# Sixteen-head attentions: values as stationary blocks of 32 columns, a turned result, and denominators summed by halvings on GpSimd

## The reference

```python
def xattn(q, k, v):                        # q: layernorm(x), k = v = context, 77 tokens
    qh, kh, vh = split(q @ Wq.T + bq), split(k @ Wk.T + bk), split(v @ Wv.T + bv)
    attn = jnp.einsum('bhqc,bhkc->bhqk', qh, kh) * 16 ** -0.5
    attn = jnp.where(mask == 0, -jnp.inf, attn)          # layer 0 alone
    attn = softmax(attn, axis=-1)
    out = jnp.einsum('bhqk,bhkc->bhqc', attn, vh)
    return merge(out) @ Wo.T + bo
x = x + tanh(g_xattn[0]) * xattn(layernorm(x), ctx, ctx)
```

## Time and profile before

| | |
|---|---|
| three runs | 1043.39, 1044.92, 1045.66 us; median 1044.92 |
| profiled execution, span | 1043.2 us |
| TensorE busy | 964.7 us (92%) |
| VectorE busy | 603.3 us (58%) |
| ScalarE busy | 489.0 us (47%) |
| GpSimd busy | 287.8 us (28%) |
| chain that ended last | TensorE 20% of the span, the last feed-forward block |

### The profile page before, as it was taken

How to read it: one execution, slowest core, us unless ns; L and a number is a source line. 1 busy time by engine, 2 the same in 40 slices (tenths; PEclk the granted TensorE clock), 3 DMA queues, 4 the chain that set the end, 5 groups by cost and what they waited for, 6 DMA issues and landing times. The chain is left out here.

```text
span 1043.2 us, 18151 instructions
## 1 busy us (share of the span) xinstructions
PE 964.7 (92%) x6476; PEld 835.3 (80%) x6477; DVE 603.3 (58%) x1253; ACT 489.0 (47%) x744; POOL 287.8 (28%) x271
## 2 busy tenths in 40 slices
PE   6999999989999999877988889999998999999997
PEld 5778878878888888565777778887885799999996
DVE  5858769951223222689898999666776522222221
ACT  3654422111111111688785878255552556656561
POOL 2000000033444442280006112600000344444442
PEclk9999999999999999998999999999999999999999
DMA  9200040025667664011000010260115223322332
GB/s 295 69 1 22 21 143 21 21 77 166 181 181 210 182 168 91 15 41 41 1 1 2 1 41 2 99 231 21 41 42 171 83 45 50 48 45 48 51 45 31
DMA packets 62500, 79.38 MB, mean 76 GB/s; under 512 B 7340, under 2 KB 46855, under 8 KB 62439
## 3 DMA queue, kind: packets, MB, share of 16 engines
q1 hardware_dynamic: 48807, 59.95, 17.0%
q0 software_dynamic: 13632, 18.62, 10.2%
HBM read 60.73 MB, written 17.83 MB: 75 GB/s over the span
## 5 line engine op out<-in xcount | busy, mean ns | idle before, releaser
L3165 PEld LDWEIGHTS ps<-room,xn_sb 128*128 128x128 f32 x1248 | 145.6, 192 | 2.7 <-issue 0.8
L3165 PE MATMUL ps<-room,xn_sb 128*128 128x128 f32 x1248 | 146.3, 275 | 0.6 <-issue 0.6
L288 POOL TENSOR_TENSOR norm_vec<-norm_vec,powers 128x4 f32<-128x4 f32 (+2 forms) x27 | 28.9, 1071 | 360.7 <-DVE norm_vec L282 360.7
L3118 POOL DMA_INDIRECT out_x<-f_yo,f_give x39 | 62.0, 1589 | 110.5 <-DVE f_yo L3363 97.5
L3234 ACT ACTIVATE xn_sb<-w_L_ffn_w 128x1024 f32 x78 | 82.1, 1057 | 20.8 <-DVE f_te L3331 10.8
L3357 DVE TENSOR_TENSOR room<-room,ps 128x512 f32<-128x512 f32 x39 | 26.8, 687 | 109.5 <-PE ps L3165 109.5
L2857 DVE TENSOR_TENSOR room<-room,ps 128x1024 f32<-128x1024 f32 x24 | 29.3, 1219 | 104.0 <-issue 89.5
L2461 PE MATMUL ps<-b_room,room 128*128 128x256 f32 x384 | 85.6, 380 | 3.7 <-DVE room L2857 1.6
L2461 PEld LDWEIGHTS ps<-b_room,room 128*128 128x128 f32 x384 | 72.6, 190 | 14.1 <-issue 1.8
L2673 ACT ACTIVATE room<-ps 128x1024 f32<-128x1024 f32 x24 | 24.6, 1023 | 115.2 <-PE ps L2441 115.2
L2418 POOL DMA_INDIRECT acc_rows<-f_eo,f_idx x32 | 52.4, 1637 | 94.7 <-DVE f_eo L2883 50.9
(11 more groups left out here) (404 smaller groups left out, 2059.4 us busy)
## 6 DMA issues: line engine op xcount, KB each, us to landing
w_L_ffn_w<-in_L_ffn_w SPq DMA_DIRECT2D x24, 512.0 KB, 9.8
b_room<-in_L_ffn_Wg SPq DMA_DIRECT2D x16, 512.0 KB
b_room<-in_L_ffn_Wu SPq DMA_DIRECT2D x16, 512.0 KB
b_room<-in_L_ffn_Wd SPq DMA_DIRECT2D x16, 512.0 KB, 6.3
xn_rows<-xn_sb SPq DMA_DIRECT2D x8, 512.0 KB, 2.9
x_sb<-in_x SPq DMA_DIRECT2D x4, 512.0 KB, 6.4
xn_sb<-in_L_ffn_w SPq DMA_DIRECT2D x2, 1024.0 KB, 7.6
x_sb<-acc_rows SPq DMA_DIRECT2D x4, 512.0 KB, 5.9
```

The source lines that it names most:

```text
L3118: pool.indirect_dma_start(out_rows[:, :], bass.IndirectOffsetOnAxis(ap=give[:, j:j + 1], axis=0), yo[j % 2][:, :], None, compute_op=ALU.ad ...
L3165: m = pe.matmul(ps[:, banks[p], f * P:(f + 1) * P], wb[p][:, n, i, f * P:(f + 1) * P], xsT[p][:, i * P:(i + 1) * P], start=(i == 0), stop= ...
```

## The change

- A head's weights are padded from 77 to 80 (`LP`), so that the 16 heads make 1280 columns, ten pieces of 128; the padding of `pr` is set to zero once.
- `values(n)` takes a block of `vblk` of 128 x 32 (two heads) as stationary and 128 columns of `pT` as moving side, and writes partitions 32i to 32i + 31 of the result. Sixteen matmuls in two phases; the late phase waits for the third eviction. The result comes out turned (features on partitions), so `turn_heads` and the copy to `oT` go away.
- The denominators no longer come from the ones. GpSimd adds the halves of `pr` per head, 80 to 40 to 20 to 10 (`denominators`, three additions over 640, 320 and 160 elements, into `sm`); VectorE sums the ten and takes the reciprocal (`inverse(n)`, first in its iteration n, ahead of `front(n+2)`); ScalarE copies the 16 reciprocals to 256 columns (`widen(n)`, behind the exponentials of n+1, ahead of the evictions of n); TensorE transposes these two blocks behind the last two of the weights, and one 128 x 512 eviction takes all four.
- `normalise(n)` is one multiplication of the result in PSUM by the turned reciprocals, straight into `oT`, which has two buffers.
- `project(n-1)` stands behind `turn(n, (0, 1))` instead of at the end of the iteration.
- Waits: the exponentials also wait for the first addition of two tiles before; the third eviction waits for the multiplication of the tile before, as `values(n)` does; `normalise(n)` waits for the projection of the tile before; `project(n)` for the residual of the tile before.
- `place_values` has 5 matmuls (128 or 256 columns) and 5 VectorE operations; `own` is masked by 2 operations of GpSimd instead of 20. The roots go between the denominators; the table `lanes` of layer 3 is filled at the end of GpSimd's program of the attention.

```diff
@@ tensor: turn, values @@
                         if r == 2:
                             pe.wait_ge(pt_sb, 3 * n + 1)
-                        elif n:
-                            pe.wait_ge(pt_sb, 3 * n)
...
+                            for half in range(2):
+                                lo = half * HALF + 4 * P
+                                pe.transpose(ps[:, 4, half * P:(half + 1) * P], pr[:, n % 2, lo:lo + P], K.ident[:, :])
+                            pe.wait_ge(r_wide, n + 1)
+                            for k in range(KT):
+                                m = pe.transpose(ps[:, 4, (2 + k) * P:(3 + k) * P], wide[:, k * P:(k + 1) * P], K.ident[:, :])
...
                 def values(n):
...
-                        pe.wait_ge(on_ready, n)
-                    for r, (lo, hi) in enumerate(rounds):
-                        pe.wait_ge(pt_sb, 3 * n + r + 1)
-                        for part in range(lo, hi):
-                            w, h = rows[part], head0[part]
-                            m = pe.matmul(ps[:, 6, h * HV:(h + 3) * HV], pT[0:w, n % 2, part, :],
-                                          vblk[0:w, n // TB, part, :, :].rearrange("p j c -> p (j c)"),
-                                          start=(part == 0), stop=(part == NC - 1), skip_group_check=True)
+                        pe.wait_ge(oT_sb, n)
+                    for late in range(2):
+                        for half in range(2):
+                            pe.wait_ge(pt_sb, 3 * n + (3 if late else half + 1))
+                            for i in range(4):
+                                q = i + late
+                                m = pe.matmul(ps[i * RG:(i + 1) * RG, 6, half * P:(half + 1) * P],
+                                              vblk[:, q, 2 * b + half, 0 if late or i == 0 else 1, :], pT[:, n % 2, half if q < 4 else 2, q if q < 4 else half, :],
+                                              start=(half == 0 and not late), stop=bool(late), skip_group_check=True)
                     m.then_inc(o_ready, 1)
...
                     turn(n, (0, 1))
                     if n:
-                        turn_heads(n - 1)
+                        project(n - 1)
...
-                    if n:
-                        project(n - 1)
@@ scalar @@
+                        act.wait_ge(s_den, 3 * (n - 2) + 1)
...
+                def widen(n):
+
+                    act.wait_ge(r_den, n + 1)
+                    if n:
+                        act.wait_ge(pt_ps, 3 * n)
+                    act.activation(wide[:, :].rearrange("p (h d) -> p h d", h=H),
+                                   rden[:, n % 2, :].unsqueeze(2).broadcast_to([P, H, HD]), ACT.Copy).then_inc(r_wide, 1)
...
+                    widen(n)
+                    for r in range(3):
                         act.wait_ge(pt_ps, 3 * n + r + 1)
                         if n >= 2 and r == 0:
                             act.wait_ge(o_ready, n - 1)
+                        if n >= 2 and r == 2:
+                            act.wait_ge(oT_sb, n - 1)
+                        act.activation(pT[:, n % 2, r, :, :].rearrange("p a b -> p (a b)"),
+                                       ps[:, 4 + r % 2, :], ACT.Copy).then_inc(pt_sb, 1)
@@ gpsimd @@
+                def denominators(n):
+
+                    def add(src, w):
+                        lo = H * (LP - 2 * w)
+                        to = sm[:, n % 2, lo:lo + H * w].rearrange("p (h k) -> p h k", h=H)
+                        pool.tensor_tensor(to, src[:, :, 0:w], src[:, :, w:2 * w], ALU.add).then_inc(s_den, 1)
+                        return to
+
+                    pool.wait_ge(p_ready, n + 1)
+                    forty = add(pr[:, n % 2, :].rearrange("p (h k) -> p h k", h=H), LP // 2)
+                    pool.wait_ge(s_den, 3 * n + 1)
+                    twenty = add(forty, LP // 4)
+                    pool.wait_ge(s_den, 3 * n + 2)
+                    add(twenty, LP // 8)
@@ vector @@
+                def inverse(n):
+
+                    lo = H * (LP - LP // 4)
+                    dve.wait_ge(s_den, 3 * n + 3)
+                    dve.tensor_reduce(den[:, n % 2, :], sm[:, n % 2, lo:lo + H * LP // 8].rearrange("p (h k) -> p h k", h=H), AX.X,
+                                      ALU.add).then_inc(s_sum, 1)
+                    dve.wait_ge(s_sum, n + 1)
+                    if n >= 2:
+                        dve.wait_ge(r_wide, n - 1)
+                    dve.reciprocal(rden[:, n % 2, :], den[:, n % 2, :]).then_inc(r_den, 1)
+
                 def normalise(n):
...
                     dve.wait_ge(o_ready, n + 1)
-                    dve.reciprocal(rden[:, n % 2, :], o[:, :, HD]).then_inc(n_step, 1)
...
+                        dve.wait_ge(y_ready, n - 1)
+                    dve.tensor_tensor(oT[:, n % 2, :], ps[:, 6, 0:D],
+                                      pT[:, n % 2, 2, 2:4, :].rearrange("p a b -> p (a b)"), ALU.mult).then_inc(oT_sb, 1)
...
                 for n in range(NT):
+                    inverse(n)
                     if n + 2 < NT:
                         front(n + 2)
```

More of the change, by code:

```diff
@@ L31 @@
 H, HD = 16, 16
-CHUNKS = -(-H * L // P)
+LP = 80
+PARTS = 5
+HALF = H * LP // 2
 LN_EPS = 1e-5
@@ L348, in multihead @@
     G2 = 2 * L
-    rounds = [(0, 4), (4, 8), (8, NC)]
+    PLACE = ((0, 6, 0), (1, 6, 128), (4, 6, 384), (2, 7, 0), (3, 7, 256))
     ps = K.ps
@@ L425, in place_values @@
                     again = K.again[:, :, :].rearrange("l h k -> l (h k)")
-                    for part in range(NC):
-                        w, h = rows[part], head0[part]
-                        m = pe.matmul(ps[0:w, 6 + part // HALF, part % HALF * 96:(part % HALF + 1) * 96].rearrange("p (b c) -> p b c", b=B),
-                                      again[:, part * P % L:part * P % L + w], vnat[:, :, h * HD:(h + 3) * HD], start=True, stop=True)
-                        if part % HALF == HALF - 1:
+                    for q, bank, at in PLACE:
+                        lo, hi = max(q - 1, 0), min(q + 1, 4)
+                        w = 4 * (hi - lo) * RG
+                        m = pe.matmul(ps[:, bank, at:at + w].rearrange("p (g c) -> p g c", g=2 * B),
+                                      again[:, q * P % LP:q * P % LP + P],
+                                      vnat[:, :, :].rearrange("l b (h c) -> l (b h) c", h=2)[:, :, lo * RG:hi * RG],
+                                      start=True, stop=True)
+                        if q >= 3:
                             m.then_inc(s_vp, 1)
@@ L489, in turn @@
                         m.then_inc(pt_ps, 1)
                 def values(n):
+                    b = n // TB
                     if n:
[L493 to L500 removed]
@@ L551, in _ @@
                 if first:
-                    pe.wait_ge(opening.again, 1)
+                    pe.wait_ge(opening.again, 2)
                 place_values()
@@ L719, in _ @@
                     opening.gpsimd(pool)
-                for b in range(B):
-                    m = pool.tensor_copy(vblk[:, b, :, :, HD].rearrange("p c j -> p (c j)"), K.own[:, :])
-                m.then_inc(s_vblk, 1)
-                for g in range(len(norm.groups)):
-                    if first or g:
-                        norm.root(pool, g)
-                if ahead is not None:
-                    ahead.gpsimd(pool)
+                pool.memset(pr[:, :, :].rearrange("p n (h k) -> p (n h) k", h=H)[:, :, L:LP], 0.0).then_inc(s_vblk, 1)
+                def denominators(n):
[10 more added lines that the diff above has]
+                    add(twenty, LP // 8)
+                if first:
+                    norm.root(pool, 0)
+                norm.root(pool, 1)
+                if ahead is not None:
+                    ahead.gpsimd_start(pool)
+                for n in range(NT):
+                    denominators(n)
+                    if first and n in (0, 2):
+                        norm.root(pool, 2 + n // 2)
+                    if ahead is not None:
+                        ahead.gpsimd(pool, n)
+                if ahead is not None:
+                    ahead.gpsimd_end(pool)
             @block.vector
@@ L1685, in rows_of_x, with gpsimd_start, gpsimd, gpsimd_end @@
         pass
-    def gpsimd(self, pool):
-        for g in range(len(self.GROUPS)):
-            self.norm.root(pool, g)
+    def gpsimd_start(self, pool):
+        pass
+    def gpsimd(self, pool, n):
+        for g, (_, hi) in enumerate(self.GROUPS[:4]):
+            if n == hi + 1:
+                self.norm.root(pool, g)
+    def gpsimd_end(self, pool):
+        self.norm.root(pool, 4)
     def vector(self, dve, n):
```

124 lines of the change are left out of this document (47 added, 77 removed).

## The result

The changed kernel takes 1054.25 us in the median of five runs (1051.89 to 1058.81) against 1045.1 for the kernel before; the ratio is 1.0089, with a 95% interval of 1.0071 to 1.0108. It is slower by some 9 us. The prediction of 1046.2 was wrong, and its range ended at 1054.0, just under the median. The profiled execution spans 1051.2 us, 8.0 more than before.

The account below looks back on a forecast made before the run. VectorE was taken to bind layer 0, with TensorE holding it up in layer 3. Terms -0.6 + 0.9 + 0.6 - 0.6 + 1.0 = +1.3; 1043.2 + 1.3 + 1.7 = 1046.2 us, range 1039 to 1054.

Parts of the forecast that it names:

- the one on GpSimd: GpSimd's halving adds beside VectorE: hidden themselves, slowing VectorE's small operations, mainly bias and moments, by +1.0 us in all.
- rival B: Layer 0's bias on VectorE waits for GpSimd's adds, up to 1.59 us each, 6 us in all: 1051; chance 0.12.
- rival C: Values on TensorE: four blocks don't all run together, late phase over 0.75, loop 0.25 longer: 1052; chance 0.21.
- Four tiles: Two plain tiles and two with extra transposes: 24.92 us for 25.12 in layer 0, 23.86 for 23.58 in layer 3.
- The loop: Per-tile cycle from inverse through ScalarE, TensorE and normalise back to the next inverse: 5.88 us, binding layer 3.
- the hops: Loop steps from inverse through widen, evictions, transposes and hand-overs to the late values phase: 3.69 us.
- VectorE's room: Layer 0 tiles: VectorE nearly always busy, so taking work off TensorE alone buys at most 0.2 us per tile.
- The tails: Each attention's last two tiles, without front: loop stays 5.88, once with moments taken at 0.9 more; +0.7 and +1.6.
- rival A: Both attentions: shorter hand-overs make the loop 5.6 us, no contention, -5.0 us in all: 1040 us; chance 0.25.
- From the last multiplication to the last residual: End of each attention: new chain 1.74 us instead of 3.71, -2.0.

Follow-up runs that it names:

- no_adds: Changed kernel without GpSimd's three halving additions per tile (one element written instead, VectorE sums ones; denominators left out): 1044.6 us, 0.9991 of the kernel before.
- rows_moved: Changed kernel with moments and normalised rows moved behind the next iteration's maximum and subtraction, roots one tile later: 1040.78 us, 0.9962 of the kernel before.
- bias_first: Changed kernel with moments and rows moved behind the next iteration's bias, and layer 3's table cast ahead of GpSimd's loop: 1035.72 us, 0.9912 of before.
- rows_two_inputs: Changed kernel with the normalised rows computed by an operation with two tensor inputs instead of one with two scalars: 1059.11 us, 1.0133 of before.

## Why the prediction was wrong, point by point

**The step that failed** is the one on GpSimd, "I take +1.0 us in all". It rests on "Only the bias (16 operations) and the moments have two operands in SBUF", and the rows were left out of the list because they have one tensor input and two columns of scalars. They stand in VectorE's order right behind the residual, where the exponentials have just ended and the additions begin; they are what the additions hit. The term measured 9.7 us (the changed kernel less `no_adds`, medians) instead of 1.0. Of the 15 us by which rows grew, 11.3 reached the end, by the residuals of both attentions.

The prediction had the mechanism as rival B, at 0.12, and gave it a price near the true one (6 us against 9.7), but tied it to the bias. The nearness is luck, as the price was worked out from 16 biases that weren't held. The bias collides just as hard when it is put there (1.77 us in `rows_moved`); it decided at another operation. The view that would have told was at hand: list VectorE's operations in the order of their start behind the end of the exponentials, for a tile with rows, and ask of each whether it could meet the addition, instead of going by operands.

The Trainium skill, "SBUF — State Buffer", section "Who interferes with whom", names the operation: beside those with two SBUF inputs it lists copies, casts and `tensor_scalar` as able to take the port pair that VectorE and GpSimd share, with whoever comes first keeping it for the whole instruction. The trace agrees (a row ends 0.15 us behind the addition's end; the row that came 0.27 ahead of one was not held). The prediction quoted half of that rule, and the half that it left out is the one that decided.

**What held.** Without the additions the forecast is 1046.2 - 1.0 = 1045.2; `no_adds` measured 1044.6. That the sum came out is in part luck, as two errors cancel in it: up to the thirteenth residual `no_adds` is 2.3 us shorter than before in layer 0 and 1.6 in layer 3 (forecast: 0.6 shorter and 0.9 longer), and behind it 3.1 and 2.7 longer (forecast: 0.3 each).
- TensorE's blocks run side by side: the 32 records of values take 1.40 us (1.3 forecast), four blocks of 32 columns at once, and the late phase 0.64 (0.65), so rival C's condition isn't met. These are the rows of after, of both phases and of the late one:

```profile
112.22 1.40 PE L503 MATMUL ps<-a_pT,a_vblk 128*32 128x128 f32 x32
...
112.98 0.64 PE L503 MATMUL ps<-a_pT,a_vblk 128*32 128x128 f32 x16
```

- The three additions take 1.55, 0.86 and 0.49, 2.9 us (2.8 forecast), and `inverse` never waits for them.
- `place_values` takes 1.91 us on TensorE (2.0).
- Four tiles in `no_adds`, from the sixth residual on: 24.71 us in layer 0 (24.92 forecast) and 23.29 in layer 3 (23.86).
- TensorE's busy share from 80 to 137 us was forecast at 85%; without the additions it is 47.29 of 57 us, 83%, and with them 79%.

**What was mis-sized.**
- The loop. The prediction read the 2.19 us from the multiplication to the next `front` off one tile and called it plain; that tile holds a pair of rows, 0.98 us. Without them it is 1.2, and with the 3.69 of the hops the loop is 4.89, which `bias_first` takes in its plain tiles. Its row of multiplication, residual, statistics and next inverse:

```profile
740.15 0.42 DVE L787 TENSOR_TENSOR a_oT<-ps,a_pT 128x256 f32<-128x256 f32 x1 [0.34 <-PE ps L503]
740.49 0.47 DVE L798 SCALAR_TENSOR_TENSOR x_sb<-ps,gates,x_sb 128x256 f32<-128x256 f32 x1
741.00 0.43 DVE L800 BATCH_NORM_STATS2 bn_st<-x_sb 128x6 f32<-128x256 f32 x1
741.34 0.30 DVE L775 TENSOR_REDUCE a_den<-a_sm 128x16 f32<-128x160 f32 x1
```

  The four-tile sums came out right, since in the changed order rows do stand in the loop.
- VectorE's room. "In layer 0 VectorE has no room" was read off the same tile. In a tile of the kernel before in which VectorE has neither rows nor moments, and TensorE has four extra transposes, VectorE idles 1.49 us from residual to residual (88.29 to 94.78), most of it at these two places:

```profile
89.67 1.44 DVE L744 TENSOR_REDUCE a_mx<-ps 128x16 f32<-128x1232 f32 x1 [0.43 <-PE ps L472]
...
94.78 0.48 DVE L770 SCALAR_TENSOR_TENSOR x_sb<-ps,gates,x_sb 128x256 f32<-128x256 f32 x1 [0.61 <-PE ps L516]
```

- The tails. The last two tiles were taken at 5.88 and 6.8. Without the additions they take 5.83 and 7.74 in layer 0 and 5.96 and 7.61 in layer 3: a pair of rows stands ahead of the last inverse, and not the moments alone. With the additions they take 7.62 and 7.20 in layer 0; there the first holds two held rows. With rows and moments moved (`bias_first`) they take 4.89 and 5.00. This error hid the gain: with the rows moved the change is worth 0.9%, which no case of the prediction held apart from rival A's 1040.
- From the last multiplication to the last residual: 143.09 - 140.97 = 2.12, forecast 1.74 (3.71 in the earlier trace rows); a pair of rows stands ahead of the last residual:

```profile
140.97 0.42 DVE L787 TENSOR_TENSOR a_oT<-ps,a_pT 128x256 f32<-128x256 f32 x1 [2.83 <-PE ps L503]
...
143.09 0.48 DVE L798 SCALAR_TENSOR_TENSOR x_sb<-ps,gates,x_sb 128x256 f32<-128x256 f32 x1
```

**What stays open.** The runs of `no_adds` lie in two groups, 1040.1 to 1040.6 and 1044.2 to 1047.4, and those of the changed kernel spread over 7 us. The half clock (next section) falls in other places from kernel to kernel, and its part in the 9 us wasn't measured by itself. A kernel without additions and with the rows moved wasn't run, so that the 8.9 us apart from the additions come from the last tiles is read off the two traces and not shown by an edit.

## What to carry to other kernels

Before work is given to an idle GpSimd, write down which VectorE operations start while it runs; those that read two tensors from SBUF may last until the GpSimd instruction ends, and so may a `tensor_scalar` or a copy with one. Move those operations to a stretch in which GpSimd rests, or put ones that aren't held into its additions, before judging the change: here the same work went from 0.9% slower to 0.9% faster by its order, about half of that because of the additions. And when a period is read off one tile, check that this tile has no work that others lack.

## What the runs showed of the hardware

- A VectorE operation of 0.41 to 0.48 us on SBUF that starts well within a GpSimd addition is not slowed in proportion: it lasts until the addition is over. With one tensor input and two scalars it ends 0.15 us behind the addition's end (a row of the changed kernel, 1.37 us), and so does a copy ahead of the loop (1.51 instead of 0.28); with two tensor inputs 0.28 behind (a row of `rows_two_inputs`, 1.51, and the bias in `rows_moved`, 1.77). A bias that starts in the last 0.11 us of an addition keeps its 0.43, and the GpSimd addition behind it takes 0.60 to 0.63 us instead of 0.49 (five times in the changed kernel).
- Not every operation on SBUF is held. The statistics of a residual, SBUF to SBUF, keep their 0.43 us inside the long addition (rows below, of after); in `bias_first` ten of the reductions of `inverse` and eleven of the reciprocals start inside an addition and keep 0.30 and 0.25.

```profile
66.45 1.54 POOL L725 TENSOR_TENSOR a_sm<-a_pr 128x640 f32<-128x640 f32 x1 [0.43 <-ACT a_pr L626]
...
66.56 0.43 DVE L800 BATCH_NORM_STATS2 bn_st<-x_sb 128x6 f32<-128x256 f32 x1
```

- A TensorE that waits can lose its clock. In layer 3 of the changed kernel TensorE sat idle for 2.77 us, for the held rows, and right after it the granted clock was 0.50, the lower of its two levels (1.2 for 2.4 GHz): the same 32 records of values took 1.93 us instead of 1.40.

```profile
739.04 0.62 PE L481 MATMUL ps<-ident,a_pr 128*128 128x128 f32 x2 [2.77 <-ACT a_pT L696]
...
740.02 1.93 PE L503 MATMUL ps<-a_pT,a_vblk 128*32 128x128 f32 x32
```

```profile
739.10:742.40 3.30, 3.30 (x39) 2.38 (x40) 1.98 (x4) 0.88 (x2) 0.00 (x0) 0.50 0.25 85
```

So a held VectorE operation can cost more than its own time: the tile with this wait took 8.34 us from residual to residual, 2.54 more than in `no_adds`, for rows that grew by 1.8. Tiles of layer 0 with held rows and a full clock took 7.15 and 7.27, 1.2 and 1.3 more than in `no_adds`, for rows that grew by 1.4 and 1.6.
